# Windowed attention softmax: the mask moves from a product to an addition, the exponential is cut in eight

## What is computed

```python
def attn_layer(x, Wqkv, qs, ksc, Wo):        # 16 heads of 64, INNER = 1024
    q, k, v = jnp.split(x @ Wqkv, 3, -1)
    q = l2norm(q) * qs                       # then rotary tables; the same for k
    ...
    sim = jnp.einsum('bhwie,bhwje->bhwij', bq, bk2) * QK_SCALE   # windows of 32 queries, 64 keys
    sim = jnp.where(mask, -jnp.finfo(sim.dtype).max, sim)
    attn = jax.nn.softmax(sim, -1)
    out = jnp.einsum('bhwij,bhwje->bhwie', attn, bv2)
    return out @ Wo

def ffn_layer(x, g, bln, W1, b1, W2, b2):
    xn = (x - mu) / jnp.sqrt(var + 1e-05) * g + bln
    a, gate = jnp.split(xn @ W1 + b1, 2, -1)
    return a * jax.nn.gelu(gate, approximate=False) @ W2 + b2

for i in range(DEPTH):                       # DEPTH = 6
    x = attn_layer(shift_tokens(x), ...) + x
    x = ffn_layer(shift_tokens(x), ...) + x
```

## Time and profile before

| | us |
|---|---|
| median of 3 runs | 1739.27 (1736.51 to 1743.57) |
| the profiled execution | 1741.98 |
| its span, first to last instruction | 1740.2 |
| TensorE busy in the span | 1666.1 (96%) |
| VectorE busy | 1381.5 (79%) |
| GpSimd busy | 1187.3 (68%) |
| ScalarE busy | 1092.9 (63%) |

### The profile page before, as it was taken

The page is one execution under the profiler, slowest core; times in us unless marked ns, Lnnn a source line. Parts: engine busy times, 40 slices in busy tenths (PEclk is TensorE's granted clock), DMA queues, the critical chain, the costliest instruction groups (busy, mean ns, idle before and its releaser), DMA issues.

```text
span 1740.2 us, 74075 instructions
## 1 busy us (share of the span) xinstructions
PE 1666.1 (96%) x31420; PEld 1210.5 (70%) x31420; DVE 1381.5 (79%) x2661; ACT 1092.9 (63%) x1943; POOL 1187.3 (68%) x1163
## 2 busy tenths in 40 slices
PE   5889999999999999999999999999999999999995
PEld 2357777777777777677777677777677777677774
DVE  4688888887888888788888788888788887788863
ACT  2256666666666666566666566666666666566653
POOL 0377777776777767676776677677677777666751
PEclk9799999999999999999999999999999999999998
DMA  3032223332223323222323222333222332222222
GB/s 106 25 93 66 68 67 79 89 76 71 66 68 81 88 68 78 68 65 69 96 71 78 70 68 63 92 78 77 71 69 66 80 87 74 74 64 66 66 61 76
DMA packets 109735, 127.86 MB, mean 73 GB/s; under 512 B 52064, under 2 KB 55648, under 8 KB 109152
## 3 DMA queue, kind: packets, MB, share of 16 engines
q1 hardware_dynamic: 109408, 123.13, 27.9%
HBM read 20.27 MB, written 2.10 MB: 13 GB/s over the span
## 4 chain that ended last, share of the span: by engine, by line
PE 89%; DVE 4%; SPq 2%; ACT 2%; DMA 2%; issue 1%; POOL 0%; ACTq 0%; DVEq 0%; POOLq 0%
PE QKb L471 21%; PE O L594 11%; PE F L499 9%; PE VTb L512 9%; PE S L471 9%; PE S L529 8%; PE S L559 5%; PE F L616 4%; PE F L628 4%; PE F L629 3%; PE S L522 2%; SPq L397 1%; DVE t L823 1%; PE F L568 1%; DMA prm<-in_params 1%
## 5 line engine op out<-in xcount | busy, mean ns | idle before, releaser
L968 POOL TENSOR_TENSOR t<-t 128x512 f32<-128x512 f32 x384 | 488.7, 1273 | 306.6 <-DVE t L823 298.7
L823 DVE TENSOR_TENSOR t<-QKb,table 128x1024 f32<-128x1024 f32 x384 | 468.8, 1221 | 156.8 <-ACT sq L668 156.3
L962 POOL TENSOR_TENSOR t<-t,rn 128x512 f32<-128x512 f32 x384 | 400.5, 1043 | 136.0 <-DVE rn L863 136.0
L471 PE MATMUL QKb<-wq_sb,x_sh 128*128 128x512 f32 x768 | 426.3, 637 | 12.4 <-DVE t L823 11.7
L668 ACT ACTIVATE sq<-QKb 128x512 f32<-128x512 f32 x384 | 230.8, 601 | 321.7 <-PE QKb L471 314.7
L499 PEld LDWEIGHTS F<-wo_sb,OT 128*128 128x128 f32 x1536 | 202.9, 193 | 89.6 <-issue 88.7
L512 PEld LDWEIGHTS VTb<-cst,t 128*128 128x128 f32 x1536 | 186.6, 141 | 104.8 <-issue 94.0
L512 PE MATMUL VTb<-cst,t 128*128 128x128 f32 x1536 | 230.6, 273 | 0.6 <-POOL t L962 0.5
L594 PEld LDWEIGHTS O<-PT,V 64*64 64x64 f32 x12288 | 199.2, 135 | 42.7 <-issue 41.8
L876 DVE TENSOR_REDUCE ss<-sq 128x16 f32<-128x1024 f32 x192 | 224.4, 1169 | 0.0
L594 PE MATMUL O<-PT,V 64*64 64x32 f32 x12288 | 219.2, 221 | 0.9 <-DVE rn L863 0.5
(11 more groups left out here) (136 smaller groups left out, 2165.9 us busy)
## 6 DMA issues: line engine op xcount, KB each, us to landing
V<-v_tok SPq DMA_DIRECT2D x1440, 64.0 KB, 2.0
wq_sb<-in_wqkv SPq DMA_DIRECT2D x36, 256.0 KB, 3.7
wo_sb<-in_wo SPq DMA_DIRECT2D x6, 512.0 KB, 5.0
xs<-xm SPq DMA_DIRECT2D x48, 64.0 KB
xs<-xm SPq DMA_DIRECT2D x48, 63.5 KB
w_sb<-in_w SPq DMA_DIRECT2D x6, 341.0 KB, 3.3
w_sb<-in_w SPq DMA_DIRECT2D x6, 192.0 KB, 3.1
y_spill<-OT SPq DMA_DIRECT2D x1, 1024.0 KB, 4.1
```

The source lines that it names most:

```text
L471: return pe.matmul(out_, x_sh[:, pr, P * tile:P * (tile + 1)], wq_sb[:, col:col + 512], start=True, stop=True)
L823: dve.tensor_tensor(t12[:, v, :, :].rearrange("p c (h d) -> p c h d", h=8), QK_ps.rearrange("p (h d) -> p h d", h=8).unsqueeze(1) .to_broa ...
L962: pool.tensor_tensor(w, w, rn[:, vv // 4, 8 * (vv % 4):8 * (vv % 4 + 1)].unsqueeze(2) .to_broadcast([P, 8, DH]), ALU.mult).then_inc(qk_nor ...
L968: pool.tensor_tensor(w, w, t12[:, v, 1, :].rearrange("p (h c d) -> p h c d", h=8, c=2)[:, :, ::-1, :], ALU.add).then_inc(add_done, 1)
```

## The change

- The mask product and its two bfloat16 constants are gone; each small score product starts its own sum.
- VectorE adds the mask (float32, from the constants) to the scores on the way from PSUM to E, and then takes the maximum of E, negated, into nmx. The banks are free after the first of the two (mask_done instead of sub_done).
- ScalarE takes the exponential in eight pieces of 64 columns, each with its column of nmx as bias.
- The three transfers of the token shift are issued from ScalarE's queue, in slot 1 instead of slot 0, behind the GELU of the third chunk. The normalisation (F_NM) is one slot later.
- w1, w2 and prm have a semaphore each. prm has two buffers and is loaded early in the layer before its use; w1 and w2 are loaded after their last product instead of after the last batch is finished.
- The order within a slot is another on TensorE, VectorE, ScalarE and GpSimd.

```diff
-F_WO, F_MID, F_SH, F_ST, F_NM, F_XT, F_AFF = 21, 24, 24, 27, 27, 29, 29
+F_WO, F_MID, F_SH, F_ST, F_NM, F_XT, F_AFF = 21, 24, 25, 27, 28, 29, 29
...
-        ident_bf = sb("ident_bf", [P, P], BF16)
-        mask_bf = sb("mask_bf", [P, 4 * KEYS], BF16)
...
-        prm = sb("prm", [P, R_ALL])
+        prm = sb("prm", [P, 2, R_ALL])
...
-                if slot == F_END + 1:
-
-                    wait(sp, ff_final, l * B)
-                    sp.dma_start(w1_sb[:, :], w1[l]).then_inc(in_ffn, 16)
-                    sp.dma_start(w2_sb[:, :, :], w2[l])\
-                      .then_inc(in_ffn, 16)
-                    sp.dma_start(prm[:, :], params[l]).then_inc(in_ffn, 16)
+                if slot == 2:
+
+                    wait(sp, ff_final, (l - 1) * B)
+                    sp.dma_start(prm[:, l % 2, :], params[l]).then_inc(in_prm, 16)
+                if slot == F_HID + 1:
+
+                    wait(sp, w1_ready, l * B * NCH)
+                    sp.dma_start(w1_sb[:, :], w1[l]).then_inc(in_w1, 16)
+                if slot == F_W2 + 1:
+
+                    wait(sp, w2_ready, l * B)
+                    sp.dma_start(w2_sb[:, :, :], w2[l]).then_inc(in_w2, 16)
...
-                    f, pr = batch(s, par, v, F_SH)
-                    if f is not None:
-
-                        wait(sp, mid_done, f + 1)
-                        wait(sp, normed, f * NT)
-                        sp.dma_start(xs[:, :, 0:D // 2], xm[:, pr, :, 0:D // 2]).then_inc(xs_moved, 16)
-                        sp.dma_start(xs[1:P, :, D // 2:D], xm[0:P - 1, pr, :, D // 2:D]).then_inc(xs_moved, 16)
-                        sp.dma_start(xs[0:1, 1:NT, D // 2:D], xm[P - 1:P, pr, 0:NT - 1, D // 2:D]).then_inc(xs_moved, 16)
...
-                        for p in range(2):
-                            pe.matmul(S2[:, p, 0:4 * KEYS], ident_bf[:, :], mask_bf[:, :], start=True, stop=False,
-                                      skip_group_check=True)
...
-                                                   start=False, stop=ct == 3, skip_group_check=True)
+                                                   start=True, stop=True)
...
                     if live(a, QUADS):
-                        wait(act, sub_done, a + 1)
-                        act.activation(E[:, k, :], E[:, k, :], ACT.Exp).then_inc(exp_done, 1)
+                        wait(act, max_done, a + 1)
+                        for i in range(8):
+                            w = E[:, k, KEYS * i:KEYS * (i + 1)]
+                            ex = act.activation(w, w, ACT.Exp, bias=nmx[:, k, i:i + 1])
+                        ex.then_inc(exp_done, 1)
...
                     f, pr = batch(s, par, v, F_HID)
                     if f is not None:
                         gelus(f, pr, [2])
+                    f, pr = batch(s, par, v, F_SH)
+                    if f is not None:
+
+                        wait(act, mid_done, f + 1)
+                        wait(act, normed, f * NT)
+                        act.dma_start(xs[:, :, 0:D // 2], xm[:, pr, :, 0:D // 2]).then_inc(xs_moved, 16)
+                        act.dma_start(xs[1:P, :, D // 2:D], xm[0:P - 1, pr, :, D // 2:D]).then_inc(xs_moved, 16)
+                        act.dma_start(xs[0:1, 1:NT, D // 2:D], xm[P - 1:P, pr, 0:NT - 1, D // 2:D]).then_inc(xs_moved, 16)
...
-                        mv_ = mx[:, k, :].rearrange("p (b c) -> p b c", b=2)
-                        dve.tensor_reduce(mv_, Sv, AX_X, ALU.max).then_inc(max_done, 1)
-                        wait(dve, max_done, a + 1)
+                        Ek = E[:, k, :].rearrange("p (c b k) -> p b c k", c=4, b=2)
                         wait(dve, pt_ready, a - 3)
                         if a == 0:
                             wait(dve, yT_done, 4)
-                        dve.tensor_tensor(E[:, k, :].rearrange("p (c b k) -> p b c k", c=4, b=2), Sv,
-                                          mv_.unsqueeze(3).to_broadcast([P, 2, 4, KEYS]),
-                                          ALU.subtract).then_inc(sub_done, 1)
+                        dve.tensor_tensor(Ek, Sv, cst[:, C_MASK:C_MASK + 4 * KEYS]
+                                          .rearrange("p (c k) -> p c k", k=KEYS).unsqueeze(1)
+                                          .to_broadcast([P, 2, 4, KEYS]), ALU.add).then_inc(mask_done, 1)
+                        wait(dve, mask_done, a + 1)
+                        wait(dve, exp_done, a - 3)
+                        dve.tensor_reduce(nmx[:, k, :], E[:, k, :].rearrange("p (c k) -> p c k", k=KEYS), AX_X, ALU.max,
+                                          negate=True).then_inc(max_done, 1)
```

More of the change, by code:

```diff
@@ L698, in step @@
                         stage(BANK_TX[:, 0:N], 1 - par)
+                    f, pr = batch(s, par, v, F_GEL)
+                    if f is not None:
+                        gelus(f, pr, [0, 1])
                     a, k, st, pr = quad(s, par, v, L_PT)
@@ L801, in step @@
                     g = s * SLOTS + v
-                    f, pr = batch(s, par, v, F_W2)
-                    if f is not None:
-                        hidden(f, pr, [2])
-                    recurrence(in_fill(s, v, 0))
                     f, pr = batch(s, par, v, F_MID)
@@ L810, in step @@
                                           ALU.add).then_inc(mid_done, 1)
+                    f, pr = batch(s, par, v, F_HID)
+                    if f is not None:
+                        hidden(f, pr, [0, 1])
+                    recurrence(in_fill(s, v, 0))
                     f, pr = batch(s, par, v, F_END)
@@ L813, in step @@
                         finish(f, pr)
-                    f, pr = batch(s, par, v, F_HID)
+                    f, pr = batch(s, par, v, F_W2)
                     if f is not None:
-                        hidden(f, pr, [0, 1])
+                        hidden(f, pr, [2])
                     if live(g, UNITS):
```

207 lines of the change are left out of this document (102 added, 105 removed).

## The result

| | before | after |
|---|---|---|
| median | 1741.03 us (1736.51 to 1743.57, 4 runs) | 2008.13 us (2006.69 to 2009.76, 4 runs) |
| span of the profiled execution | 1740.2 us | 2004.9 us |
| mean granted clock of TensorE | 0.985 | 0.91 |
| TensorE, VectorE, GpSimd, ScalarE busy | 96, 79, 68, 63% | 88, 69, 60, 65% |

The changed kernel is slower: the ratio is 1.1538, with a 95% interval of 1.1509 to 1.1567. The forecast was 1938 us with a range of 1765 to 2005. Its direction was right, its range ended 3 us short.

A forecast was written before the change was run, and what follows sets the result against it. TensorE was taken to bound the kernel, busy for 1666.1 of 1740.2 us. 1742 + 147 - 2 + 18 - 19 + 55 = 1941, less 2.7 us to the median: 1938 us, range 1765 to 2005.

The forecast's parts named there:

- weight semaphores: Layer boundaries: TensorE's 13.4 us of waiting for parameters and 2 us for each of three clock falls go, -19 us.
- mask product: TensorE, ahead of the scores: dropping it saves 0.31 us per quad, 0.93 per batch for three of the four.
- issues and exponentials on ScalarE's chain, small stalls: Slot 2: issues hold ScalarE 4.32 us, eight exponentials take 1.87 instead of 0.54; with 0.4 us stalls per batch, +208 us.
- the new order: Moves of W2, WO and PT's transposes, and of VectorE's and GpSimd's work: costed at nothing.
- clock: TensorE's granted clock falls in the new wait, a mean of 1.2 us per batch: +55 us, between 0 and 101.
- The GELU: ScalarE, ahead of the issues: 0.47 us more if it must finish first; counted only in the range's upper end.
- The exponentials: ScalarE: one of 64 columns takes 328 ns, spacing 0.234 us, eight take 1.87 us until the next instruction.
- The chain of slot 2: From slot 2's query/key product to slot 3's scores: 9.9 us, before 5.75, so 4.1 us more per batch.
- The lower end: Mask product worth 0, if the scores' first weights wait as long behind the transposes as the mask product took.
- the reading in which every batch pays 2 us: Clock, by the Trainium skill: every batch starts at the low clock, 92 us, making the sum 37 us higher.
- Short issues: Rival: each issue takes about 0.7 us on ScalarE, holding it 2.2 us; +51 us, 1787 us; chance 0.16.
- No hold at all: Rival: issuing occupies only the queue and ScalarE goes on; -12 us from the chain, 1724 us; chance 0.14.

The follow-up runs named there:

- e_b_sems: The kernel before with own semaphores for w1, w2 and prm, prm in two buffers, loaded as in the changed kernel; 1719.83 us, ratio 0.9880.
- e_b_nomask: The kernel before with the mask product left out and no mask applied; 1711.51 us, ratio 0.9833.
- e_fill4: The changed kernel with idle TensorE products, four behind PT's transposes of slot 2 and three behind slot 3's projection; 1946.21 us, ratio 1.1185.
- e_sp_one_exp: The changed kernel with token-shift transfers on SyncE and one exponential instead of eight, the maximum taken but not subtracted; 1710.79 us, ratio 0.9839.
- e_b_exp8: The kernel before, its order and SyncE transfers kept, with own weight semaphores, mask added on VectorE and eight exponentials; 1755.95 us, ratio 1.0092.
- e_b_rowmax: The kernel before with own weight semaphores, mask added on VectorE and one exponential with one negated maximum per row; 1689.36 us, ratio 0.9714.
- e_sp: The changed kernel with the three token-shift transfers issued from SyncE's queue again, in slot 1; 1758.84 us, ratio 1.0116.
- e_tiny_first: The changed kernel with the one-row transfer of the token shift issued before the 127-row one; 1833.50 us, ratio 1.0554.

## Why the prediction was right in direction and short in size

Each term of the sum, in us over the whole kernel. Measured are differences between kernels of the table. The parts depend on each other, so two terms have two values: the first with the new order put in ahead of the eight exponentials, the second with the exponentials first.

| step of the forecast | forecast | measured | from |
|---|---|---|---|
| weight semaphores | -19 | -20 | e_b_sems |
| mask product | -45 | -28 | e_b_nomask |
| issues and exponentials on ScalarE's chain, small stalls | +208 | +235 or +254 | e_fill4 less e_sp_one_exp; or e_b_exp8 less e_b_rowmax (67) and after less e_sp, less the clock (187) |
| the new order | 0 | +19 or +3 | e_sp_one_exp less 1691.8; or e_sp less e_b_exp8 |
| clock | +55 | +62 | after less e_fill4 |
| sum | +199 | +268 or +271 | |

The mechanism was right and three sizes fell short: ScalarE's chain by 27 to 46 us, the mask product by 17, the order by 3 to 19. In either sequence the largest is ScalarE's chain. The time missed the range by 3 us; with the first or the second size right it would have lain inside.

**Who is held, and by what: right.** The issue rows came out as forecast (0.68, 0.74 and 2.80 us, against 0.67, 0.76 and 2.72 in the earlier trace rows), and ScalarE stood still for them. The GELU, 0.47 us long, did not have to finish first: the first issue starts 0.06 us after the GELU's start. The square came at 4.79 us instead of 4.52, with 0.06 for that start and the rest in a third issue of 2.94 us.

**The exponentials: right.** A single one takes 336 ns (forecast 328), eight follow each other at 0.24 us (0.234), and KT's copy starts 1.92 us after the first (1.87).

**The chain of slot 2: its end right to 5%, its start taken from an unusual batch.** Scores at 10.35 us, forecast 9.9; in e_fill4, at full clock, 10.03. But the forecast measured from 5.75, and the usual batch before takes 5.54. The chain made the usual batch longer by some 4.5 us, not by 4.1: over 46 batches this is some 18 us of what the term lacks.

**The step that failed: the size of ScalarE's chain.** The sum had +208 us for issues, exponentials and small stalls; it was 235, or 254. Besides the start of 5.75, it took 2.76 us for every third issue, though on SyncE's queue the longest had been 3194 ns. Chain of the changed kernel at a boundary:

```profile
736.06 5.45 ACTq L711
...
748.03 1.53 PE F L516 x12
```

Here it took 5.45 us, and that batch 42.07 us. At the five boundaries the third issue took 4.72, 5.45, 3.96, 5.12 and 4.70 us, and in the batch behind each 3.4 to 3.9, which makes 14 us over its median of 2.80. What holds the queue there was not tested. The rest of the term was not taken apart.

**The mask product: mis-sized.** "The rows show the full 0.31 between two starts on a busy engine, so I take it" was the step, with 45 us in the sum. They show when the next instruction started, not when it could have started without this one. The lower end was named for exactly this reason; a value between the ends would have been right. The 45 count three products per batch, since the fourth lies behind ScalarE's chain; the 28 are for all four in a kernel without that chain.

**The new order: put at nothing, and not nothing.** "The waits that they could save are not there" was true, but the step asked only what the moves could save, not which wait they could make. PV lost the 0.6 us of PT's transposes ahead of it and met the Newton steps, 0.70 us per batch. In the changed kernel PV waits as long (935.41 above), but the order's price there was not measured under the hold; with eight exponentials and the transfers on SyncE it is 3 us.

**The clock: the size right, the way to it partly luck.** 62 against 55. The forecast had the clock fall in three batches of five, at 2 us each; in the trace it fell in nearly every batch, at 1.35 us each. The 92 us of the reading in which every batch pays 2 us were too many.

**The rivals.** Short issues are what e_tiny_first has made of the kernel, 0.68, 0.64 and 0.72 us: 1833.5 us where 1787 had been worked out, 46 short, for which mask product and order would account with 20 to 36 by the table. No hold at all, 1724 as forecast, is e_sp with 1758.8: it would not have been a gain. The Trainium skill, "DMA: Bandwidth & Descriptors", section "Anatomy of one DMA — SWDGE (gpsimd) path", puts the dispatch at about 50 ns; on ScalarE's queue in this kernel the shortest of 144 issues took 661 ns. That section is on the path of GpSimd, and its figure does not carry over to these queues: the measurement decides.

The range was too narrow at its upper end. It summed two ends, of the clock and of the GELU, but not two others that the prediction had itself named: the mask product worth nothing (+45 us) and small stalls of 0.8 us (+18). And it left the other moves without an end at all. Two of the prediction's small figures do not agree with its own numbers, without consequence: 1883 + 101 + 22 is 2006, and the hold at which nothing is gained or lost is given as 1.1 us in one place and 1.3 in another.

## What to carry to other kernels

An engine that both computes and issues transfers stood still for each issue here, 0.7 to 2.8 us and 5.45 at most, and its busy share doesn't show it; put issues on an idle queue, and a short transfer ahead of a long one, not behind. Eight small instructions for one cost 1.4 us here, whatever the share of the engine says: what counts is the slack in the slot where it is nearly late. When work is moved on the bounding engine, ask of the instruction that comes earlier now what it waits for. And compare several batches before taking a slack from one: here the batch that was read had 0.40 us and the usual one 0.19.

## What had not been expected of the hardware

- The issue of a one-row transfer took 0.64 us ahead of, and 2.80 us behind, a transfer of 127 rows; 3.96 to 5.45 us there at the layer boundaries.
- Work without use made the kernel faster by 62 us: seven idle products per batch kept TensorE's granted clock at its upper level, 2.4 GHz, through its waits.
- What an instruction costs depends on its neighbour: the scores, in small tiles, follow the transposes after 0.53 us, the mask product after 0.44. The mask product was also in bfloat16, so whether the tile or the type makes the 0.09 us is not shown.
